# One ring of eight buffers for two kinds of load, in place of four and four, in a 16-channel convolution kernel

## What is computed

```python
# layer 0: per-channel 6x11 convolution of the lower triangle
xm = jnp.where(causal_mask, gn(x), 0)
y  = conv_general_dilated(xm, weight, padding=((5, 0), (5, 5)), feature_group_count=16)
x  = x + jnp.where(causal_mask, y, 0)
# layer 1: a bias that depends on row - column alone
x  = x + (gn(x) + bias[c, row - column])
```

## Time and profile before

| | |
|---|---|
| median of 3 runs (lowest to highest) | 2722.15 us (2718.95 to 2722.83) |
| the profiled execution: time, span | 2720.33 us, 2718.5 us |
| busy share of the span: PE, DVE, ACT, POOL | 73%, 85%, 61%, 46% |
| DMA packets in the two queues, share of 16 engines | 58.6% (SP's) and 30.6% (ACT's) |
| moved | 901.17 MB, mean 331 GB/s |

### The profile page before, as it was taken

How to read it: one execution, slowest core, us unless ns; L and a number is a source line. 1 busy time by engine, 2 the same in 40 slices (tenths; PEclk the granted TensorE clock), 3 DMA queues, 4 the chain that set the end, 5 groups by cost and what they waited for, 6 DMA issues and landing times. The chain is left out here.

```text
span 2718.5 us, 76785 instructions
## 1 busy us (share of the span) xinstructions
PE 1986.9 (73%) x28880; PEld 1885.9 (69%) x28880; DVE 2307.3 (85%) x4175; ACT 1661.5 (61%) x3051; POOL 1247.5 (46%) x1988
## 2 busy tenths in 40 slices
PE   4299978777787878877678777877768777989500
PEld 0199978777777767877678777777768777879400
DVE  7799988898889988899788998899888996969825
ACT  2177766756576656766567665666657665777521
POOL 1133254545445355544555455454544535655533
PEclk9999999998899989999889988999989998999855
DMA  9756569998899988999799998999889996979899
GB/s 338 274 197 201 192 216 408 357 374 313 325 409 353 367 326 339 399 348 359 293 394 384 353 353 303 405 365 371 323 330 401 354 358 222 351 269 344 303 337 347
DMA packets 316250, 901.17 MB, mean 331 GB/s; under 512 B 42416, under 2 KB 42416, under 8 KB 314000
## 3 DMA queue, kind: packets, MB, share of 16 engines
q1 hardware_dynamic: 199648, 579.79, 58.6%
q10 hardware_dynamic: 116416, 319.37, 30.6%
HBM read 579.50 MB, written 319.68 MB: 331 GB/s over the span
## 5 line engine op out<-in xcount | busy, mean ns | idle before, releaser
L1131 PEld LDWEIGHTS psY<-wsplit,XT 128*128 128x128 f16 x25920 | 1612.4, 102 | 313.7 <-DVE XT L751 116.5
L1131 PE MATMUL psY<-wsplit,XT 128*128 128x168 f16 (+5 forms) x25920 | 1638.1, 223 | 252.5 <-DVE XT L751 217.0
L611 ACT CAST XT<-psT 128x512 f16<-128x512 f32 x720 | 414.5, 576 | 534.6 <-PE psT L1117 316.4
L751 DVE TENSOR_TENSOR XT<-psT,XT 128x512 f16<-128x512 f32 x720 | 493.3, 685 | 191.8 <-ACT XT L611 190.0
L1031 POOL TENSOR_TENSOR xn<-xn,mask 128x512 f32<-128x512 f32 x336 | 440.6, 1311 | 423.4 <-ACT xn L599 364.4
L1117 PE MATMUL psT<-ident,xn 128*128 128x128 f32 x2880 | 486.9, 294 | 177.1 <-POOL xn L1031 136.7
L1066 POOL TENSOR_TENSOR ubuf<-ubuf,bias 128x1024 f32<-128x1024 f32 x184 | 413.5, 2248 | 375.6 <-ACT ubuf L658 375.1
L1057 POOL COPY halo<-XT 128x16 f16<-128x16 f16 x720 | 300.9, 418 | 611.9 <-DVE XT L751 598.9
L779 DVE BATCH_NORM_STATS2 entries<-abuf 128x6 f32<-128x512 f32 x872 | 549.0, 678 | 29.1 <-DMA abuf<-in_x 28.9
L1117 PEld LDWEIGHTS psT<-ident,xn 128*128 128x128 f32 x2880 | 321.8, 148 | 187.9 <-POOL xn L1031 121.6
L599 ACT ACTIVATE xn<-kept_c_band,normp 128x512 f32<-128x512 f32 (+2 forms) x496 | 398.4, 803 | 33.3 <-DMA kept_c_band<-in_x 17.0
(11 more groups left out here) (78 smaller groups left out, 464.1 us busy)
## 6 DMA issues: line engine op xcount, KB each, us to landing
abuf<-in_x SPq DMA_DIRECT2D x436, 512.0 KB, 8.1
out<-ubuf ACTq DMA_DIRECT2D x288, 512.0 KB, 6.2
kept_c_band<-in_x SPq DMA_DIRECT2D x224, 512.0 KB, 8.5
out<-kept_c_band ACTq DMA_DIRECT2D x224, 512.0 KB, 6.9
ubuf<-in_x SPq DMA_DIRECT2D x192, 512.0 KB, 7.1
band<-in_x SPq DMA_DIRECT2D x48, 1024.0 KB, 9.1
out<-band ACTq DMA_DIRECT2D x48, 1024.0 KB, 9.9
ubuf<-out SPq DMA_DIRECT2D x96, 512.0 KB, 8.6
```

Of the source, the lines that this page charges most:

```text
L611: nc.scalar.copy(XT[:, n % NB3, 0, :, 2:P + 2], psT[n % NB3][:, :, :]).then_inc(hi_ready, 1)
L751: nc.vector.tensor_tensor(XT[:, n % NB3, 1, :, 2:P + 2], psT[n % NB3][:, :, :], XT[:, n % NB3, 0, :, 2:P + 2], ALU.subtract).then_inc(lo_r ...
L1131: last = nc.tensor.matmul(psY[m][:, 0:rows, o + lo_c:o + hi_c], XT[:, m, xp, i, 2 - sh:2 - sh + P], wsplit[:, c, wp, K * sh:K * sh + rows, ...
```

## The change

`abuf` and `ubuf` become one `ring` of the same size, eight buffers of 512 KB. All loads of both kinds are merged into one list, sorted by the position at which they are wanted, and load k takes buffer k % 8. Before it SP waits for whatever held that buffer: the statistics of an a unit or the landed store of a u unit. A streamed unit is wanted three positions ahead of its use (14 in the last pair) in place of two; a statistics unit still two. Positions of use follow from the merged list. The number of instructions of each kind on each engine stays as it is, and so do the positions of all other DMAs, and the four-buffer order of the first pair's statistics.

```diff
-    NAB, NUB = 4, 4
+    NAB, NRING = 4, 8
...
+    A_LEAD, U_LEAD, LAST_LEAD = 2, 3, 14
+    planned = {}
+    wanted = [(max(NT * g + at, NT - 1), "a", g, a) for g in range(1, G) for a, at in enumerate(STEADY.a)]
+    for g in range(G):
+        p = plan(g + 2 < G, g + 1 < G, True, on_dve)
+        lead = U_LEAD if g + 1 < G else LAST_LEAD
+        planned.update({(g, u): at for u, at in enumerate(p.u)})
+        wanted += [(NT * (g + 2) + max(at - lead, 0), "u", g, u) for u, at in enumerate(p.u)]
+    wanted.sort()
...
+    for k, (at, kind, g, i) in enumerate(wanted):
+        key, n = (kind, g, i), k % NRING
+        load = max(at, load, free_at[n])
+        buffer_of[key], held_by[key], in_buffer[n] = n, in_buffer[n], key
+        loads[n] += 1
+        load_count[key] = loads[n]
+        loads_at.setdefault(load, []).append(key)
+        if kind == "a":
+            use[kind] = min(max(load + A_LEAD, use.get(kind, 0)), NT * g + A_END)
+            free_at[n] = use[kind] + 1
+        else:
+            hi = U_WINDOW[CPG * i // NU][1]
+            use[kind] = max(NT * (g + 2) + planned[(g, i)], load + A_LEAD, use.get(kind, 0))
...
+            stored = min(use[kind] + (1 if on_dve[i] else 2), NT * (g + 3) - 1)
...
+            free_at[n] = stored + 1
...
+            def load_unit(key, u, src):
+
+                kind, g, i = key
+                n, held = buffer_of[key], held_by[key]
+                if held and held[0] == "a":
+                    wait_alone(sp, a_done, a_base(held[1]) + held[2] + 1)
+                elif held:
+                    wait_alone(sp, u_stored[n], 16 * store_count[held])
+                sp.dma_start(unit_of(ring, n, u), part(src[chan(g, u[0]), u[1]], u)).then_inc(ring_loaded[n], 16)
```

More of the change, by code:

```diff
@@ L181, in preact_conv_kernel @@
                 at = kept_pos[blk][1] + 1
[L183 to L188, removed]
     def plan(do_a, do_b, do_c, on_dve=None):
@@ L344, in preact_conv_kernel @@
         scale_chain = sem("scale_chain")
-        a_loaded = [sem(f"a_loaded{i}") for i in range(NAB)]
+        ring_loaded = [sem(f"ring_loaded{i}") for i in range(NRING)]
         a_done = sem("a_done")
@@ L358, in preact_conv_kernel @@
         u_finished = sem("u_finished")
-        u_stored = [sem(f"u_stored{i}") for i in range(NUB)]
+        u_stored = [sem(f"u_stored{i}") for i in range(NRING)]
         kept_done = sem("kept_done")
@@ L483, in stage @@
                 for n in range(NT):
[L484 to L489, removed]
+                    for key in units_at(loads_at, "a", s, n):
+                        load_unit(key, A_STREAM[key[2]], xv)
                     if do_b:
@@ L707, in stage @@
                             shift_bias(gc, 1, NV)
-                        for u in range(NU):
-                            if p.u[u] == n and not on_dve[u]:
-                                scale_stream(gc, u)
+                        for _, g, u in units_at(uses_at, "u", s, n):
+                            if not on_dve[u]:
+                                scale_stream(g, u)
                         for blk in KEPT:
@@ L722, in _ @@
                 act.wait_ge(half_stored, 16 * G)
-            for i in range(NUB):
-                act.wait_ge(u_stored[i], 16 * G * (NU // NUB))
+            for i in range(NRING):
+                act.wait_ge(u_stored[i], 16 * stores[i])
             for s in x1_spilled.values():
@@ L986, in stage @@
                                     finish_kept(gc, blk, h)
-                        for u in range(NU):
-                            if p.u[u] == n and on_dve[u]:
-                                finish_stream(gc, u)
-                    for g, a in a_items(p.a, s, n, do_a, do_next):
+                        for _, g, u in units_at(uses_at, "u", s, n):
+                            if on_dve[u]:
+                                finish_stream(g, u)
+                    for _, g, a in units_at(uses_at, "a", s, n):
                         stream_stats(g, a)
@@ L1086, in stage @@
                     if do_c:
-                        for u in range(NU):
-                            if p.u[u] == n and not on_dve[u]:
-                                add_bias(gc, u)
+                        for _, g, u in units_at(uses_at, "u", s, n):
+                            if not on_dve[u]:
+                                add_bias(g, u)
             stages(stage)
```

103 lines of the change are left out of this document (54 added, 49 removed).

## The result

The changed kernel takes 2641.79 us (median of 4 runs, 2639.70 to 2644.11) where the kernel before takes 2722.28 (4 runs, 2718.95 to 2722.83): ratio 0.9707, 95% interval 0.9690 to 0.9724. It is 80 us faster.

A forecast was written before the change was run, and what follows sets the result against it. Steady stages of 320 us were bound by no single engine (DVE 285, DMA 279), with 35 us from late units. Terms 18 + 19 - 18 - 2 + 2 + 12 = 31 us gave 2691 us, eight-in-ten range 2660 to 2726.

The forecast's parts named there:

- sign of being wrong: Steady stages, forecast at about 317 us, moving by more than 8 us either way would show the prediction wrong.
- place 2: Steady stages, u12 to u17: a29 and a33 wait for streamed units' stores; 3 us lost per stage, 18 in all.
- Place 1: Steady stages, u5 and a15: ACT's wait for u5 goes, DVE waits 4.3 us for a15; counted as nothing.
- both waits felt: The losing end for u5 and a15 in a steady stage: -4 us per stage.
- a48: Steady stages: its load moves from position 56 to 54, ahead of kept reloads; 3 us gained per stage, 18 in all.
- The end of the stage: Steady stages: DVE's waits for u33 and u35 both go; 3.24 us gained per stage, 19 in all.
- Stage 8: Stage without statistics, 249 us: more buffers for streamed units gain 2 of the 31 us in which PE is not busy.
- Stage 9: Last stage, phase C alone: eight units loaded before the first finishes; 12 us gained, at most 26.
- First stage: Eight statistics units of pair 1 move from stage 0 to stage 1: 2 us lost, between 0 and 10.
- faster, more than forecast: Chance 0.16: SP runs further ahead wherever either kind alone is dense, filling the thin parts; about 2655 us.
- Bandwidth decides: Chance 0.14: transfers can't be faster over a stage, so steady stages keep 320 us and the last its time; 2720 us.
- Slower: Chance 0.16: statistics units wait for streamed units' stores, holding up DVE; 2755 us. Sign: DVE's statistics waits grow over 60 us.

The follow-up runs named there:

- two pools: Changed kernel's merged order and leads, but four buffers each for statistics and streamed units again, sharing undone: 2725.4 us, 1.0026 of the kernel before.
- two runs: u5 loaded one position earlier in the kernel before: 2720.6 us; a15 loaded and used three positions earlier in the changed kernel: 2638.9 us.
- lead 2: Changed kernel with streamed units wanted two positions ahead of use in place of three: 2650.4 us, 0.9745 of the kernel before.
- ring of seven: Changed kernel with one of its eight ring buffers left unused: 2728.7 us, 1.0036 of the kernel before.
- the run with the earliest free buffer: Changed kernel, but each load takes the buffer planned to be free first, not the one used eight loads before: 2625.5 us, 0.9665.

## Why the prediction was wrong

The sign was right, with 0.70 on faster; the size was not: 31 us for 80. The steady stages moved by 9.0 us each, beyond the 8 that I had named as a sign of being wrong. The step that failed is the pricing of the shared buffers. I went through the single waits where both kinds are dense, and counted there 3 us lost per stage, where 0.2 were; the rest got too little: stage 8 got 2 us and gained 10.4, stage 9 got 12 and gained 18.7, and positions 66 to 84 got nothing and gained 2.4 a stage. By the terms of the sum:

- **Places 1 and 2.** Counted at 0 and -3 per stage, measured -2.4 (a gain) up to position 24 and +2.6 (a loss) from 24 to 48: together +0.2 where 3 lost were forecast, 17 us of the miss. The size of the loss at place 2 was right and the way partly: two pools, in which no statistics unit waits for a store, lose 1.5 us there as well, so the waits for stores that I had named can be only part of it. In the trace a33 is late by 2.4 us as argued, a29 by 0.3 and not 3.4, u12 by 3.9 for 1.9, and u16, which I held to be not helped, has lost its 4.3 us. Place 1 went as described, but "both waits felt" had no meaning: two runs show that a wait there is paid back by position 24. What does keep 2.4 us is not shown. It is gone with lead 2 (+0.1), with two pools (+0.5) and with the ring of seven (+1.9), and by position 24 of stage 5 the changed kernel has moved 28.7 MB (56.2 us at 343 and 24.2 at 391 GB/s) and the kernel before 29.5 (59.7 at 330 and 24.0 at 410), so part of it may be bytes put off to the next piece.
- **a48.** Forecast 3, measured 3.1 alone and 2.7 in the changed kernel: right. But 2.4 us more are gained at positions 66 to 84, which I counted at nothing. Less the 0.3 by which a48 fell short, this is 13 us of the miss. They come with the new order, in two pools as well (2.5), and by what wait stays open: the longest one there, ACT's 3.2 us a stage for u28, is still 2.2 in two pools. A part is work moved elsewhere: ten statistics units are used at positions 67 to 84 in both runs, where the kernel before used twelve, and one more each at 25 to 48 and at 85 to 90, at 1.29 us of DVE a unit.
- **The end of the stage.** "So both waits of 1.6 us go: 3.24 per stage": they went, and 4.2 was measured, so the term is 1 us too small. Against the new order without sharing it is 6.6, since the order alone brings 2.4 of loss there. I compared with the kernel before and didn't ask what the denser order would cost without the ring. PE's wait was not shorter, as forecast, but earlier.
- **Stage 8.** "I take 2 of the 31 us": measured 10.4, the term furthest off for its size. In that stage ACT waited 8.5 us for units and DVE 3.0 in the kernel before, and both are gone; no term of mine held them. Part of the gain needs the lead: with lead 2 the stage is 245.9 us, and ACT waits 3.8 us for a unit again.
- **Stage 9.** "I take 12, about half": measured 18.7 of the 26 that the rate of the earlier trace rows allowed. The mechanism was right, that eight units in flight fill the gaps. It runs at 388 GB/s with a share of 0.99, and the second bias is issued 69 us into the stage, for 79 before.
- **First stage.** +2 forecast, +5.2 measured, inside its bounds.

The sum of the differences is 2.8 + 2.1 + 1.0 per stage, 35 us, then 8 and 7 in stages 8 and 9, less 3 at the start: 47 of the 49 missed; the rest lies between the medians and the profiled executions.

Of the rivals, "faster, more than forecast" is what happened, further than its 2655: the ring lets SP run ahead where one kind alone is dense. I had named the mechanism and priced it by the waits of places 1 and 2, where it does nothing; it acts where one kind is thin or absent, at the stage's end and in stages 8 and 9. "Bandwidth decides" is true of one stretch, behind place 1, and not of the stage. "Slower" had its waits (DVE's for statistics units grew by 29.5 us, short of the 60 that I named) and not their price. It describes the ring of seven in part: the largest loss lies where it put it, at place 2, but there ACT waits 5.8 us a stage for u12 and 6.2 for u16, and DVE only 3.0 for a33. The Trainium skill ("DMA: Bandwidth & Descriptors", Specifications) gives an HBM limit of about 358 GB/s for a core, half of what it gives a stack. This trace of a one-core program goes beyond it, with 365 over a steady stage and 388 over the last.

## What to carry to other kernels

Buffers split between two uses should be shared where the uses are dense at different times: look for the stretches where one kind is thin or absent, and price those and not the places where both are busy. Don't tie a shared buffer to its turn when one kind holds it much longer than the other: take the one that is free first, or an earlier load can slow everything behind it. A wait removed ahead of a stretch at full DMA rate (410 to 417 GB/s here) was paid back in it, in two runs; ahead of a slower one (348 GB/s) most of it was kept, in one.

## What was not expected of the hardware

Over whole stages the DMA engines hold rates near the peak of short stretches: 388 GB/s over 144.8 us of reads and writes, and 393 GB/s over 78 us in this window of the run with the earliest free buffer, positions 24 to 48 of stage 5:

```profile
1395.80:1473.90 78.10, 65.07 (x983) 62.04 (x980) 69.13 (x129) 56.72 (x99) 42.10 (x69) 0.96 1.01 393
```

The mean granted clock of the profiled executions was 0.901 in the ring of seven (2728.7 us), 0.905 before, 0.919 in the changed kernel and 0.921 with the earliest free buffer. No run separates the clock from the waits, so how much of each gain is the clock's stays open. In stage 9, where PE does next to nothing (0.59 us), the changed kernel gains 18.7 us all the same.
